# Graph layer with residual and normalisation: x held still, 320 count columns streamed, both source halves in one buffer

## The reference

```python
m_data = x[src] @ W_data.T + b_data
m_ctrl = x[src] @ W_control.T + b_control
msg = where((edge_type == 0)[:, None], m_data, m_ctrl)
agg = segment_sum(msg, dst, num_segments=12500)
h = relu(agg + (x @ W_self.T + b_self))
y = x + h
out = (y - mean(y)) / sqrt(var(y) + 1e-5)      # over the 128 features
```

## Time and profile before

| | |
|---|---|
| median of three runs | 2256.65 us |
| profiled execution, first to last instruction | 2255.3 us |
| TensorE matmul busy | 2108.4 us, 93% |
| VectorE busy | 1193.7 us, 53% |
| ScalarE busy | 1412.6 us, 63% |
| GpSimd busy | 1540.4 us, 68% |
| mean granted TensorE clock | 0.988 |

### The profile page before, as it was taken

The page is one execution under the profiler, slowest core; times in us unless marked ns, Lnnn a source line. Parts: engine busy times, 40 slices in busy tenths (PEclk is TensorE's granted clock), DMA queues, the critical chain, the costliest instruction groups (busy, mean ns, idle before and its releaser), DMA issues.

```text
span 2255.3 us, 65825 instructions
## 1 busy us (share of the span) xinstructions
PE 2108.4 (93%) x26955; PEld 1866.0 (83%) x26955; DVE 1193.7 (53%) x3465; ACT 1412.6 (63%) x2452; POOL 1540.4 (68%) x1632
## 2 busy tenths in 40 slices
PE   2899999999999999999999999999999999999998
PEld 2788888888888888888888888888888888888887
DVE  7654555554555555545555555455455555554543
ACT  5566666666666666666666666666666666665664
POOL 6377767767767676677776776766767776766662
PEclk9999999999999999999999999999999999999999
DMA  7422222222222222122222221222122212221210
GB/s 212 107 61 62 60 59 57 62 56 61 57 58 59 59 58 60 53 61 57 61 57 56 60 60 52 61 58 59 54 59 57 60 55 59 59 60 54 59 55 25
DMA packets 110265, 140.75 MB, mean 62 GB/s; under 512 B 39165, under 2 KB 83100, under 8 KB 109962
## 3 DMA queue, kind: packets, MB, share of 16 engines
q0 software_dynamic: 52640, 107.91, 16.9%
q1 hardware_dynamic: 57322, 28.57, 4.7%
HBM read 127.33 MB, written 9.03 MB: 60 GB/s over the span
## 4 chain that ended last, share of the span: by engine, by line
PE 76%; DVE 7%; issue 5%; ACT 5%; DVEq 4%; SPq 1%; DMA 1%; POOL 0%; ACTq 0%; POOLq 0%
PE apply_ps L656 43%; PE build L638 13%; PE sum_ps L620 8%; ACT cnt L833 4%; DVEq L1127 4%; DVE acc L1133 2%; PE misc L706 2%; PE misc L665 2%; PE misc L684 1%; DVE hot_q L1100 1%; PE misc L709 1%; PE misc L708 1%; PE misc L707 1%; PE misc L671 1%; DMA key_dram<-x_u 1%
## 5 line engine op out<-in xcount | busy, mean ns | idle before, releaser
L555 POOL DMA_INDIRECT rows<-in_x,src_t x1570 | 1489.8, 949 | 644.1 <-issue 400.7
L833 ACT ACTIVATE cnt<-build 128x784 fp32r<-128x784 f32 x1568 | 1205.7, 823 | 750.2 <-PE build L638 726.6
L656 PE MATMUL apply_ps<-x,cnt 128*128 128x258 f32 x9604 | 1366.9, 292 | 18.1 <-DVE sd L1153 17.3
L656 PEld LDWEIGHTS apply_ps<-x,cnt 128*128 128x128 f32 x9604 | 1235.3, 193 | 51.6 <-issue 36.7
L1100 DVE TENSOR_TENSOR hot_q<-const_ps,key_pq 128x784 bf16<-128x784 bf16 x784 | 432.0, 556 | 84.8 <-PE build L638 72.5
L638 PE MATMUL build<-hot_q,hot_p 64*128 64x98 bf16 x12544 | 451.6, 208 | 23.4 <-ACT cnt L833 14.3
L638 PEld LDWEIGHTS build<-hot_q,hot_p 64*128 64x128 bf16 x12544 | 317.2, 95 | 148.8 <-ACT cnt L833 24.1
L1131 DVE TENSOR_TENSOR acc_deg<-misc,acc_deg 2x32 f32 x314 | 56.2, 179 | 534.9 <-PE misc L665 426.7
L1096 DVE TENSOR_TENSOR hot_p<-const_ps,key_pq 128x1024 bf16<-128x1024 bf16 x392 | 268.2, 684 | 88.2 <-PE build L638 74.0
L620 PE MATMUL sum_ps<-rows,hot 128*64 128x129 f32 x3140 | 211.9, 280 | 3.1 <-DMA rows<-in_x,src_t 3.1
L620 PEld LDWEIGHTS sum_ps<-rows,hot 128*64 128x64 f32 x3140 | 171.8, 137 | 18.1 <-DMA rows<-in_x,src_t 4.6
(11 more groups left out here) (174 smaller groups left out, 959.9 us busy)
## 6 DMA issues: line engine op xcount, KB each, us to landing
rows<-in_x,src_t POOLq DMA_INDIRECT x1570
cnt_raw<-in_x SPq DMA_DIRECT2D x13, 448.0 KB, 7.4
x_u<-in_x SPq DMA_DIRECT2D x48, 64.0 KB
out<-y_sb SPq DMA_DIRECT2D x48, 64.0 KB
key_dram<-x_u SPq DMA_DIRECT2D x16, 160.5 KB
x_u<-in_x SPq DMA_DIRECT2D x36, 53.5 KB
out<-y_sb SPq DMA_DIRECT2D x36, 53.5 KB
win_i<-in_dst SPq DMA_DIRECT2D x25, 64.0 KB
```

The costliest lines, as they stand in the source:

```text
L555: pool.indirect_dma_start(out=rows[:, slot, 0:D], out_offset=None, in_=x, in_offset=bass.IndirectOffsetOnAxis(ap=src_t[:, col:col + 1], ax ...
L656: last = pe.matmul(apply_ps[:, 0:ROW + 2], cnt[:, half, i, :], x2[:, b, :], start=(b == 0), stop=(b == XBLOCKS - 1))
L833: act.activation(o, i.rearrange("p h (m b) -> p b h m", b=HALF), ACT.Copy).then_inc(evacuated, 1)
```

## The change: what it does

The roles in `apply` are exchanged. A 128 x 128 block of x2 (rounded part, then rest) is now stationary, and 320 count columns, that is 160 nodes with two types, are moving. There are 40 groups (`DGROUPS`) of 160 nodes, so the dense way covers 6400 nodes and the gather way 154 rounds. For a group there are 98 x blocks with two parts: 196 matmuls of 320 columns, 7840 in all, in place of 9604 of 258. The result has features on partitions, so no transposition of a block is needed: `take_fin` on VectorE copies 320 columns from `apply_ps` into `fin`, 40 times.

A *pass* is one half of one group: ten batches of 16 nodes (`TURNS` = 10), 80 passes, 800 batches. Both halves of the sources share the one buffer `cnt`. A batch of half 1 is written into the place that ten steps before was read by the apply of half 0; for this, half 1 has the turned layout (`counts`, `counts_of`), so that what apply(a) reads is what evacuate(a + 10) overwrites. Each step has one run of 10 matmuls (8 in the last of a pass), ahead of the build: `apply(s - 10)`. Its first run of a pass waits for the evacuation of the last batch, which was built in the step before.

`hot_p` is built for every batch, in a ring of two. On VectorE `make_onehots` stands ahead of `add_sums` and `take_out`, and works two batches ahead, not three. Degrees of dense nodes no longer come from columns of ones: `prepare_keys` counts them, and `turn_keys` has two small matmuls more. `hot` and `sg` have one buffer each. Output units of the dense way are 128, 128 and 64 nodes of every 320; there are 114 units in the loop, before 104, and four at the end. x goes straight to its place, loaded from ScalarE's DMA queue; the three edge lists are loaded first; key groups 1 and 2 have a table of the first two chunks. GpSimd's waits on `built` are gone.

```diff
-    gather_step = [(BATCHES + APPLY_AT) * r // PAIRS for r in range(PAIRS)]
+    slots = [0] + [10 * p + o for p in range(PASSES) for o in (4, 9)][:-1]
+    gather_step = [slots[i * (len(slots) - 1) // (PAIRS - 1)] for i in range(PAIRS)]
...
+        def counts(q, half):
+            if half:
+                return turned[:, :, 2 * NODES * q:2 * NODES * q + 2 * NODES]
+            return cnt[:, COLS * q:COLS * q + COLS].rearrange("p (j c) -> p j c", j=TURNS)
...
             for ps in range(PAIRS):
...
                 for i in range(2 * GT):
-                    if ps >= AHEAD and i and FIFTH[i] != FIFTH[i - 1]:
-                        n = gather_step[ps - AHEAD] + FIFTH[i]
-                        if n < BATCHES:
-                            pool.wait_ge(built, 2 * (n + 1))
...
-            def apply(y, c):
-                k, half = divmod(y, 2)
-                if c == 0:
-                    pe.wait_ge(evacuated, 8 * (y + 1))
-                    if half == 0 and k:
-                        pe.wait_ge(posted, k)
...
-                for i in range(b0, b1):
-                    b = half * HALF + i
-                    last = pe.matmul(apply_ps[:, 0:ROW + 2], cnt[:, half, i, :], x2[:, b, :],
-                                     start=(b == 0), stop=(b == XBLOCKS - 1))
+            def apply(a):
+                t, r = divmod(a, TURNS)
+                G, half = divmod(t, 2)
+                blocks = [half * HALF + q for q in dense_rows(r, half)]
+                if r == 0:
+                    pe.wait_ge(evacuated, 2 * TURNS * (t + 1))
+                    if half == 0 and G:
+                        pe.wait_ge(fin_taken, G)
...
+                for b in blocks:
+                    for k in range(2):
+                        last = pe.matmul(sums, x2[:, b, D * k:D * k + D], counts(b - half * HALF, half),
+                                         start=(b == 0 and k == 0), stop=(r == TURNS - 1 and half == 1
+                                                                          and b == blocks[-1] and k == 1))
+                last.then_inc(applied, 1)
...
-            def turn_block(k):
-                pe.wait_ge(posted, k + 1)
-                pe.matmul(misc[0:2, P:P + 64], zd[:, :], picks[:, 1, :], start=True, stop=True)
-                pe.transpose(misc[:, 0:P], sd[:, :], ident[:, :]).then_inc(misc_full, 1)
...
             for s in range(STEPS):
-                y, c = divmod(s - APPLY_AT, 4)
-                if c == 0 and 0 < y <= 2 * BLOCKS:
-                    apply(y - 1, 4)
+                if apply_at(s) is not None:
+                    apply(apply_at(s))
                 if batch_at(s) is not None:
                     build(batch_at(s))
...
             def evacuate(n):
-                y, q4 = divmod(n, 4)
-                if q4 == 0 and y >= 2:
-                    act.wait_ge(applied, y - 1)
+                t, r = divmod(n, TURNS)
+                if t:
+                    act.wait_ge(applied, TURNS * (t - 1) + r + 1)
...
             def make_onehots(n):
-                if n >= 3:
-                    dve.wait_ge(built, 2 * (n - 2))
+                if n >= 2:
+                    dve.wait_ge(built, 2 * (n - 1))
...
-                if half == 0:
-                    dve.tensor_tensor(
-                        hot_p[:, 4 * q4:4 * q4 + 4, :, :], table_p...
+                dve.tensor_tensor(
+                    hot_p[:, s:s + 4, :, :], table_p...
...
             for s in range(STEPS):
-                if posted_at(s) is not None:
-                    post(posted_at(s))
+                if s in fin_at:
+                    take_fin(fin_at[s])
+                if batch_at(s + 2) is not None:
+                    make_onehots(s + 2)
...
                 if sums_at(s) is not None:
                     add_sums(sums_at(s))
...
-                if s in hot_at:
-                    make_hot(hot_at[s])
-                if batch_at(s + 3) is not None:
-                    make_onehots(batch_at(s + 3))
+                if s in gather_at and gather_at[s] + 1 < PAIRS:
+                    make_hot(gather_at[s] + 1)
```

More of the change, by code:

```diff
@@ L95, in gnn_resnorm @@
         for i in range(k):
-            t, o = ((9, 10), (11, 15), (19, 23))[i]
-            wanted.append((end + t, Unit(cut[i], cut[i + 1] - cut[i], end + t, end + o, False, e % 2, cut[i] - base)))
-    tail_wanted = [w for w in wanted if w[1].n0 == DENSE - P or w[0] >= sum_step[-1] + 5 and not w[1].dense]
+            wanted.append((end + 2 + 2 * i, Unit(cut[i], cut[i + 1] - cut[i], 0, 0, False, e % 2, cut[i] - base)))
+    tail_wanted = [w for w in wanted if w[1].dense and w[1].n0 >= DENSE - COLS + P
+                   or not w[1].dense and w[1].n0 >= WIN_0 + EPOCH_NODES * (EPOCHS - 1)]
     ends = [w[1] for w in tail_wanted]
     TAIL = len(ends)
-    assert TAIL == 4 and ends[0].dense and not any(v.dense for v in ends[1:])
+    assert TAIL == 4 and ends[0].dense and ends[1].dense and not any(v.dense for v in ends[2:])
     units = []
-    for s, v in sorted((w for w in wanted if w not in tail_wanted), key=lambda w: w[1].out):
-        s = place(max(s, units[-1].turn + 1 if units else 0))
-        units.append(v._replace(turn=s, out=place(max(s + 1, v.out, units[-1].out + 1 if units else 0))))
+    for s, v in sorted((w for w in wanted if w not in tail_wanted), key=lambda w: w[0]):
+        turn = place(max([s] + [u.turn + 1 for u in units[-1:]] + [u.out + 1 for u in units[-2:-1]]))
+        first = max(turn + 1, units[-1].out + 1 if units else 0)
+        gaps = [t for t in range(first, first + TURNS // 2) if t % TURNS == TURNS - 1 and t not in taken]
+        units.append(v._replace(turn=turn, out=place(gaps[0] if gaps else first)))
     assert all(b.turn > a.out for a, b in zip(units, units[2:]))
@@ L676, in turn_keys @@
                 pe.transpose(misc[:, 0:P], key_n[:, 0, :, :].rearrange("p h e -> p (h e)"), ident[:, :])
[L677 to L678 removed]
+                pe.transpose(misc[:, P:2 * P], key_n[:, 1, :, :].rearrange("p h e -> p (h e)"), ident[:, :])
+                for h in range(2):
+                    last = pe.matmul(misc[0:9, 2 * P + P * h:3 * P + P * h], deg_c[:, h, :], ident16[:, :],
+                                     start=True, stop=True)
+                last.then_inc(misc_full, 1)
             def turn_x(i):
@@ L804, in split_hi @@
[L804 to L811 removed]
+                act.wait_ge(x_loaded[c], 16 if c < XCH - 1 else 32)
@@ L864, in normalise @@
                                ).then_inc(out_ready, 1)
+            for c in range(XCH):
+                load_x(c)
             store_lists(0)
```

529 lines of the change are left out of this document (280 added, 249 removed).

## The result

The changed kernel takes **2251.6 us** (median of 10 runs, 2249.8 to 2253.3), the kernel before 2257.6 beside it (10 runs, 2255.7 to 2262.8): ratio 0.9968, 95% interval 0.9958 to 0.9978. It is faster by 6 us where the forecast had 30. The time lies inside the forecast's range, but the gain is a fifth of what was forecast, and the missing 24 us have to be found.

What follows compares the result with a forecast made beforehand. TensorE, busy 93% of the span, was taken to bound the kernel, by its instructions in a row plus the waits between. The terms summed to -30 us, from 2256.65 to 2226, with a range of 2145 to 2275.

Steps and rivals of the forecast that it cites:

- Start and end: First build and last steps: earlier edge lists some -6, ten steps at each end less hidden; together -4 us (-20 to +15).
- no change: Rival: evacuation lag stays and pass ends cost 0.6 more each; half of that gives 2255 us; chance 0.08.
- The apply matmuls: TensorE's apply: 7840 matmuls of 320 columns at 0.147 us replace 9604 at 0.120; term 0 us (-107 to +16).
- the load sets the pace: Rival on TensorE's apply: weight load or handover sets the 0.120, so 320 columns cost at most 0.136; 2140 us; chance 0.15.
- Steps and builds: TensorE: 16 more builds and runs, at 0.48 + 0.19 us each: +10.7 us.
- units: Output units on TensorE: 114 in the loop, before 104, +12 us; bias product of a dense unit in one short pass, -3.
- The blocks' turn: TensorE's 98 block turns (-19.6 us) and the waits before them go; take_fin's copies on VectorE are hidden: sum -39 us.
- ScalarE's lag: Build's 38.4 us wait for cnt at short runs goes, as all runs outlast the 1.54 us evacuation; 5 left: -33 us.
- End of a pass: 80 times apply waits for the evacuation of the batch built one step before: +20 us (+10 to +50).
- Key groups: prepare_keys on VectorE gets five small operations; TensorE's waits and work for 24 key groups: +10 us (0 to +35).
- VectorE otherwise: hot_p built 800 times, not 392, adds 279 us to VectorE, covered by TensorE's step; job waits +8 and -7: 0 us.
- VectorE falls behind: Rival: VectorE's step work ends too late for TensorE's build two steps on; 2282 us; chance 0.17.

Runs made afterwards that it cites:

- experiment 2: The changed kernel with the 14 loads of x issued by SP in place of ScalarE: 2232.3 us.
- Experiment 3: The changed kernel with three loads of x ahead of the first store of lists on ScalarE and eleven behind it: 2237.6 us.
- experiment 4: experiment 2's kernel plus a second buffer for the key table's chunks: 2224.1 us; then also prepare_keys two steps ahead of turn_keys, not one: 2190.7 us.
- experiment 6: keys_two_ahead with apply's stationary operand cut to the first 64 of 128 columns of x, so output not the kernel's: 2167.7 us.
- before_even_b: The kernel before with portions 12, 12, 12, 6, 7 in place of 6, 12, 12, 12, 7: 2237.0 us.
- before_both: The kernel before with portions 12, 12, 12, 6, 7 and prepare_keys two steps ahead of turn_keys in place of one: 2191.2 us.
- keys_two_ahead: The changed kernel with x loaded by SP, a second key-chunk buffer, and prepare_keys two steps ahead of turn_keys in place of one: 2190.7 us.

## Why the prediction was wrong, by its own steps

**Start and end, -4: this step failed.** Its sentence on the first build, "some -6, bounds -15 to +10, since 14 loads of x now share the queues", weighed the loads only as traffic. What they cost was ScalarE's own time: no activation starts in the 31.6 us in which it issues them, so the lists are stored late. SP had issued them before, so this cost came in with the change, and the sum has no term for it. The first build came 10.4 later instead of 6 earlier, which is 16.4 of the missing 24, and the ten steps behind it, with gathers that went out late, lost the 7.0 of experiment 2. With the loads on SP the kernel is 2258.2 - 2232.3 = 25.9 faster than the kernel before; the 4 us to the forecast's 30 are the first build, at 38.4 and so 1.9 earlier, not 6. Experiment 3 shows that it is the order on the queue, not the bytes.

The sentence on the key table, that "no gather has to wait for all 15 before group 3", was true of the gathers and missed the engine: the chunks stand ahead of the keys in VectorE's order, and each waited for the store of the one before. But this is no part of the 24, since the kernel before paid it as well. From the start of the first build to that of build 30 it takes 101.1 us, the changed kernel 107.2, experiment 2 100.0. The 90.1 of experiment 4 is a gain that the forecast did not have.

The rest of the sum came out: from the first build to the end the kernel before takes 2215.0, experiment 2 2192.1, which is -22.9 where the sum without its -6 has -24. That this is so close is in part luck, as some terms below are off by about 5 in both directions. The rival "no change" had 2255, nearer to the result than the forecast, but by the lag and the pass ends, and neither happened: the lag went, and the pass ends cost less than reckoned. "Faster" was to be below 2252, and 2251.6 meets that by a hair.

**The apply matmuls, 0: right.** 147 ns was forecast and measured (median of 7048 gaps inside runs). The rival that the load sets the pace is refuted twice, by the 147 and by experiment 6. By the Trainium skill, "TensorE: Matmul & The Clock Gate", section "Back-to-back issue gap", the matmul would take an estimated 136 ns or, as a pair with its load, under 131 (its figure for 512 columns); neither is what this kernel shows.

**Steps and builds, +10.7; gathers, -4; units, +9: right as far as seen.** The pieces stand in the timeline at their old lengths; the median of ten matmuls to the next build is 1.66 us, as reckoned.

**The blocks' turn, -39: right as far as seen.** The turns and the waits for `sd` are gone, and the only wait for `take_fin`'s result is 0.7 us, once, in an output.

**ScalarE's lag, -33: right in kind, about 5 too much, and wrong as a merit of the change.** The build's wait for `cnt` fell from 38.4 to 8.5. But the 38.4 of the earlier trace rows is 14.3 of the matmuls and 24.1 of the weight loads. From start to start the matmuls inside a build take 0.394 us before, 0.360 now and 0.359 in before_even_b, so the lag cost 27.8 in 784 builds. The same fall comes from another order of the portions in the old kernel, worth 22. Take the lag out of the prediction's sum and +3 is left: 0 + 10.7 - 39 - 4 + 12 - 3 + 20 + 10 - 4; without the +10 of the keys, whose wait both kernels of the comparison have lost, -7. Measured are -0.5 (before_both against keys_two_ahead), and this with the second buffer on the new side alone. Against the new kernel stand the 15.3 us for `misc`, where before_both has 2.2: its VectorE adds the sums behind the one-hots.

**End of a pass, +20: right in kind, 5 too much.** 14.9 us in 48 waits, where 14 in 46 and 6 were reckoned.

**Key groups, +10: right in size.** 42.0 in 21 waits from 36.7. That is 2.0 a wait, 1.7 without the 7.1 in the start, where 1.8 was reckoned for 24. (The terms shown for it add up to 1.3 to 2.3, not 1.5 to 2.3.) The cause was where VectorE's order puts the keys, which either kernel could have changed.

**VectorE otherwise, 0: right in the main loop.** 1475 us busy; "about 1450" was said, while the term's own 279 on 1193.7 gives 1473. The eight waits of TensorE for `hot_q` end by 127 us, in the start. The rival in which VectorE falls behind did not come.

## What to carry to other kernels

A DMA is not free for the engine that issues it: many large loads at the head of a queue cost that engine's first work (31.6 us of ScalarE here), and with it all that hangs on it; put them behind the first small step, or on an engine that has nothing to do. When an engine waits at many places for work that another does just too late, ask whether that work can stand one step earlier in the other's order: moving `prepare_keys` by one index was worth 33 us, where the rewrite as it stood brought 6. And before a gain is put down to a redesign, ask whether the term that carries it (here the short run) can be had in the old design by a constant.

## What was not expected of the hardware

ScalarE's loads of 448 KB: the first three issues take 0.45 to 0.6 us each, the next six 3 to 5, the last five 1.9 to 1.5; no activation starts in these 31.6 us. SP, which issues the same loads in experiment 2 in 0.4 to 2.3 us each, has nothing to compute.

A warm stream of float32r matmuls, each with weights of its own, costs 121 ns for 258 columns and 147 for 320 (medians of 8822 and 7048 gaps): 0.42 ns a column, and 13 to 14 over the columns at 2.4 GHz. Half the weights change nothing in the 147, so this surplus is not the load.

The same program took 2252 us on one chip and 3920 on another, and the kernel before 2258 and 2656. DMA packets took as long on both (median 27 ns in SP's queue and 64 in GpSimd's); the gaps have no releaser in the trace. TensorE is idle for more than 4 us 147 times there, 4 times on the first chip, and the mean granted clock is 0.79 in place of 0.99. The comparison there (after slower by 48%) is the reverse of the one that was asked for, and can't be explained from these runs.
